# When the second attention tile's decay takes its PSUM bank: ahead of the loop's opening projection or behind it

## The reference

```python
x = x + attention(layernorm(x))       # q, k, v, alpha, beta from x; k normalised
#   cla    = cumsum(log(alpha + 1e-6)) within a chunk
#   decay  = exp(cla - cla^T), lower triangle
#   attn   = (q k^T) * beta^T * decay;  y_local = attn v
#   delta  = v^T (k * beta * exp(cla_end - cla))
#   y_glob = (q state) * exp(cla);      state = state * exp(cla_end) + delta
x = x + ffn(layernorm(x))             # out = (gelu(x Wg^T) * (x Wu^T)) Wd^T
#   Wg, Wu: 4096 x 512, Wd: 512 x 4096, each = LUT[4-bit code] * scale per 32
```

## Time and profile before

| | us |
|---|---|
| median of 3 runs | 1144.14 |
| lowest, highest | 1144.07, 1144.46 |
| the profiled execution | 1143.82 |
| span of its trace | 1141.8 |

### The profile page before, as it was taken

One profiled execution on the slowest core, in us unless ns is written; L12 is line 12 of the kernel. 1 busy time (PEld: TensorE's weight loads), 2 busy tenths in 40 slices (PEclk: granted clock), 3 DMA queues, 4 the chain that ended last, 5 costly groups with the idle time before them and its releaser, 6 DMA issues.

```text
span 1141.8 us, 19963 instructions
## 1 busy us (share of the span) xinstructions
PE 1136.0 (99%) x8014; PEld 787.4 (69%) x8014; DVE 694.8 (61%) x1284; ACT 446.1 (39%) x1037; POOL 535.3 (47%) x530
## 2 busy tenths in 40 slices
PE   9999999999999999999999999999999999999999
PEld 5666655565467777777777777777777777777776
DVE  7788656367777855665566556655665566555334
ACT  4433334253344434343434343434343434343332
POOL 3386535155883945363536363635362536253110
PEclk9999999999999999999999999999999999999999
DMA  8021011000101010101010101010101010100111
GB/s 303 3 76 46 29 38 38 10 10 2 56 19 38 20 37 20 38 19 38 20 37 20 38 19 38 20 38 19 38 20 37 18 38 22 34 17 16 38 38 65
DMA packets 22828, 41.97 MB, mean 37 GB/s; under 512 B 2704, under 2 KB 3024, under 8 KB 22736
## 3 DMA queue, kind: packets, MB, share of 16 engines
q1 hardware_dynamic: 22736, 40.70, 11.3%
HBM read 36.46 MB, written 4.23 MB: 36 GB/s over the span
## 4 chain that ended last, share of the span: by engine, by line
PE 96%; POOL 1%; DVE 1%; ACT 0%; issue 0%; DMA 0%; SPq 0%; DVEq 0%; ACTq 0%; POOLq 0%
PE ps L518 45%; PE ps L558 29%; PE ps L348 8%; PE ps L479 7%; PE ps L314 1%; PE ps L440 1%; PE ps L423 1%; PE ps L447 1%; PE ps L434 1%; PE ps L358 1%; PE ps L414 1%; DMA WR<-wqkv 0%; POOL bigA L1302 0%; DVE wf L1122 0%; POOL kn_s L1327 0%
## 5 line engine op out<-in xcount | busy, mean ns | idle before, releaser
L558 PE MATMUL ps<-WR,ihl_s 128*128 128x512 f16 x768 | 184.7, 379 | 0.0
L518 PE MATMUL ps<-XT,WR 128*128 128x256 f16 x1344 | 183.3, 273 | 0.0
L518 PE MATMUL ps<-REG,WR 128*128 128x256 f16 x1344 | 183.3, 273 | 0.0
L1139 DVE TENSOR_TENSOR load<-load,ps 128x256 f32<-128x256 f32 x168 | 70.7, 421 | 179.8 <-PE ps L518 101.3
L558 PE MATMUL ps<-WR,vv 128*128 128x512 f16 x708 | 171.4, 379 | 0.0
L518 PEld LDWEIGHTS ps<-REG,WR 128*128 128x128 f16 x1344 | 131.5, 98 | 39.1
L814 ACT COPY load<-ps 128x256 f32<-128x256 f32 x168 | 62.6, 372 | 245.1 <-PE ps L518 245.1
L1139 DVE TENSOR_TENSOR bigB<-bigB,ps 128x256 f32<-128x256 f32 x168 | 70.6, 420 | 124.3 <-ACT bigB L814 93.2
L518 PEld LDWEIGHTS ps<-XT,WR 128*128 128x128 f16 x1344 | 131.5, 98 | 15.4
L814 ACT COPY bigB<-ps 128x256 f32<-128x256 f32 x168 | 62.6, 373 | 172.0 <-PE ps L518 172.0
L558 PEld LDWEIGHTS ps<-WR,ihl_s 128*128 128x128 f16 x768 | 75.2, 98 | 66.5
(11 more groups left out here) (180 smaller groups left out, 1793.6 us busy)
## 6 DMA issues: line engine op xcount, KB each, us to landing
load<-codes SPq DMA_DIRECT2D x48, 256.0 KB
load<-scales SPq DMA_DIRECT2D x48, 256.0 KB
y<-X SPq DMA_DIRECT2D x15, 256.0 KB, 2.0
bigA<-cla SPq DMA_DIRECT2D x14, 256.0 KB, 3.0
X<-x SPq DMA_DIRECT2D x3, 1024.0 KB, 13.2
WR<-wqkv SPq DMA_DIRECT2D x2, 1024.0 KB, 9.6
X<-x SPq DMA_DIRECT2D x4, 256.0 KB, 3.9
WR<-wqkv SPq DMA_DIRECT2D x4, 256.0 KB, 4.3
```

The lines of the kernel that those rows point to most:

```text
L518: mm = eng.matmul(half_bank(kind, name), w(wp, kt), x(xp, kt), start=(first and n == 0), stop=(n == 5), skip_group_check=True)
L558: mm = eng.matmul(PS[bank][:, :], ih[:, ip, 128 * tt:128 * tt + 128], buf[:, wp, 8 + j, :], start=(j == 0 and p == 0), stop=(j == end and ...
L1139: eng.tensor_tensor(c, c, half_bank(kind, end), ALU.add).then_inc(s_comb, 1)
```

## The change

The taking of the bank is split from the decay's products. `decay_bank(T)` takes the bank (and places the wait that goes with it), `decay(T)` makes the products. `decay_bank(0)` stands directly ahead of `decay(0)`, where the taking was before. `decay_bank(1)` stands behind `head(0)` and ahead of the first fill, while `decay(1)` stays behind that fill.

```diff
             def decay(T):
-                s = T % 2
-                bank = bank_of["dec", T] = banks.take(pe, (s_dec, T + 1))
+                s, bank = T % 2, bank_of["dec", T]
...
+            def decay_bank(T):
+                bank_of["dec", T] = banks.take(pe, (s_dec, T + 1))
...
             qkv("q", 1, 1, gates_sum)
+            decay_bank(0)
             decay(0)
             for T in range(NT):
                 i, fill = T - APART, fills(T)
                 head(T)
+                if T == 0:
+                    decay_bank(1)
                 for f in fill:
                     qkv(*f)
                     if f == fill[0] and T == 0:
                         decay(1)
```

## The result

The changed kernel takes 1147.44 us (median of 9 runs, 1145.97 to 1148.31); the kernel before, run beside it, 1144.20 us. The ratio is 1.0026, 95% interval 1.0018 to 1.0034 (it is not the quotient of the two medians, which would be 1.0028). By the medians the change makes the kernel slower by 3.2 us, more than the forecast of 1.9 us and outside its range. The runs of the changed kernel fall into two groups. Four have a granted clock of 1.000 and lie at 1145.97 to 1146.62 us; five have a clock of 0.997 to 0.999 and lie at 1147.44 to 1148.31 us. All 33 runs of the kernel before that stand beside the first experiments have 1.000.

The account below looks back on a forecast made before the run. TensorE was taken to bound the kernel, busy 1136.0 of 1141.8 us. 1143.82 + 0 - 0.75 + 0.75 + 1.85 = 1145.67 us, plus 0.32 for the median, given as 1146.0; range 1143.8 to 1146.6 us.

Parts of the forecast that it names:

- Step 1: Opening projection at 59.85 also waits for the eviction of `k 1 0` from ps7, done 1.16 us early: cost 0.
- the head start: TensorE reaching `head(1)`'s L414 0.75 us sooner, at 67.41 in place of 68.16, because its wait for L959 goes.
- Step 2: `head(1)` no longer waits for VectorE's eviction L959; L414 starts at 67.41 in place of 68.16, 0.75 us ahead.
- Step 3: Behind `head(1)`, `q 1 2` now waits for ps7's eviction, over 0.7 us before it is reached: cost 0.
- Step 4: `mid(1)`'s L440 waits for VectorE's L1023, which cannot move up, so the 0.75 us gained are lost again: sum 0.
- Step 5: Around `head(1)`, GpSimd's chain comes 0.14 us earlier, takes the port lock before VectorE, and delays L440 by 1.85 us.
- rival A: The forecast itself, +1.85 us: in the second tile GpSimd's L1333 starts ahead of VectorE's L1098; chance 0.45.
- the ninth tile: Stretch at 158 to 165 us where GpSimd came first: 6.69 us against the second tile's 4.84, difference 1.85 us.
- rival E: TensorE idles about 2.8 us before L440's counterpart, its clock falls to the lower level: 1152.6 us; chance 0.05.
- the wrong row: The first 10 us of the trace, 2.08 us idle at clock 1.00, taken as speaking against a clock fall.
- the whole 6.56 us stretch: TensorE's work like that from L414 at 68.16 to L434 at 74.72, assumed to take twice as long at lower clock.
- The chances of no change and of slower: Whole-kernel time within 0.2% of before, chance 0.87; slower by over 0.2%, above 1146.4 us, chance 0.11.

Follow-up runs that it names:

- the first experiments: Four variants of the changed kernel: early start undone, GpSimd held, TensorE kept busy with transposes, and L442 held with GpSimd held; the kernel before had 1144.08 us beside them.
- the deferral: Second block of codes dequantised later, in tiles 1 to 3: 1143.44 us on the kernel before, 1142.83 us on the changed kernel.

## Why the prediction was wrong

- Step 1 (the added wait costs nothing) was right: the projection still follows its forerunner at once, and taking the head start back brings 1143.98 us with the added wait in place.
- Step 2 (0.75 us ahead) was right in kind. The start, 67.25, is even 0.91 us earlier than 68.16. The idle time listed in the rows counts from the modelled end of L440, and the next step can follow its start by 0.90 us.
- Step 3 (the wait handed on is covered) was right: no wait ahead of L348 at 69.55.
- Step 4 (the head start is swallowed by VectorE) was right; with GpSimd held, the stall stood in front of L442 with 0.92 us and the time was that of the kernel before.
- Step 5 (GpSimd's chain moves up and takes its turn) was right in its mechanism and in what it costs: L1103 of 1.26 us, and L442 1.85 us later for a forecast of 1.85. Holding GpSimd removed exactly this. The shift itself was mis-sized. L1330 came at 69.83, 0.25 us earlier than before, for a forecast of 0.14 and outside its bounds of 0 and 0.23; no 0.09 us lay between it and the end of L1364. That made no difference, since L1334 (71.25 by the same count) still fell inside L1092 and ended with it, and L1335 came at 71.49 for a forecast of 71.48. So the 0.03 us that rival A seemed to hang on were set by the end of L1092 and not by the size of the shift; the three profiles of the changed kernel and the one with transposes all show the late step, 1.26 us. The match with the ninth tile carried the forecast; a copy of the same instructions elsewhere in the trace, with the offsets that the change was about to produce, gave the price that was then measured.
- The step that failed is rival E: the sum put the fall of the clock at nothing, and the range left it out. E named the mechanism and the place (about 2.8 us idle ahead of L440's counterpart, then a stretch at the lower level), and gave it a chance of 0.05 and a price of 6.56 us. Measured, TensorE stands for 0.71 + 1.88 = 2.59 us, the clock fell in 17 of 26 runs of the changed kernel, and the fall costs 1.1 to 1.6 us: by the medians of the two groups 1147.80 against 1146.25 in the first set, 1147.14 against 1146.01 in the second, and 1.6 us in the two profiles. The runs with a clock of 0.997 cost more, up to 1148.80 us. Since more than half of the runs have it, it belonged in the sum; with 1.4 us, a figure known only from these runs, that gives 1144.20 + 1.85 + 1.4 = 1147.45.
- The reason for the low chance was the wrong row. The 2.08 us of idle time in the first 10 us stand at the very start, 1.75 us of them ahead of TensorE's first instruction; they do not show what standing in the middle of work does. The reason for the high price was that the whole 6.56 us stretch was doubled, while the lower level lasted for part of L442, for L449 and for the transposes only. No row at the lower level lay in the trace of before, so the chance ought to have been open, and the range ought to have reached one such stretch above A.
- The chances of no change and of slower (0.87 and 0.11) hung on it too: without the clock the kernel would have lain at 0.16%, inside the bound of 0.2%, and with it it lies at 0.26%. The interval of 0.18 to 0.34% still holds the bound, so that it lies above 0.2% is likely but not shown.

What stays open: why the same kernel at the same place loses the clock in some runs and not in others. In one set of six runs all lost it, in another, on another chip, five of eleven kept it; whether the chip matters was not tried. TensorE's rows in the two traces show no difference: from the start of `mid(0)`'s last step L442 comes after 11.28 us where the clock holds and after 11.27 us where it falls.

## What to carry to other kernels

A stall that is removed on the bounding engine is worth only what the next wait leaves of it, and the engines released earlier may meet others in a new order: before moving a wait, compare the starts of GpSimd's and VectorE's instructions behind it, and look for a place in the trace where the order that would result already stands. Where a forecast makes TensorE stand for a few us where it did not stand before, price a share of the runs at the lower clock, even if the trace of before never shows that level. A change that only shifts a stall is worth trying again once the work that took up its gain has moved: here the swap cost 1.9 us alone, with the clock held, and gave 0.6 us (medians) to 0.8 us (traces) with the deferral.

## What the runs showed of the hardware

- Standing for 2.17 us in one piece cost TensorE's clock in 7 of 11 runs, 3.20 us in 3 of 5, 4.84 us in 3 of 3; 0.71 and 1.88 us with eight matmuls between them, in 17 of 26; 0.92 us, in 0 of 10. With most of the 0.71 and 1.88 us filled with transposes whose results nobody reads, it was 0 of 11. The counts come from different chips, so they do not rank the lengths.
- The fall need not come while the engine stands: in the last profile of the changed kernel the granted clock is 1.00 from 76 to 78 us, where TensorE hardly works, and 0.50 from 79 us on, where it is busy again.
- A shift of GpSimd's small step by 0.27 us (from 71.52 to 71.25) decided whether a step of VectorE on 128 x 512 integers took 0.42 or 1.26 us. The Trainium skill, "SBUF — State Buffer", section "Who interferes with whom", has it that whoever starts first keeps the shared ports for its whole instruction. The trace agrees: L1338 starts at 72.80, L1103 at 72.86, and L1103 is the one that takes 1.26 us. It adds that GpSimd can come in between two steps that VectorE has back to back: L1338 started while L1098 (72.48 to 72.93) was still running, took the 1.04 us that it takes elsewhere too, and L1103 came behind it.
